# Attention and a linear layer on one core: the order in front of the first exponentials, the way the heads' output goes back, and the order of the last four heads

## The reference

```
Q, K, V = split_heads(xn @ wq.T), split_heads(xn @ wk.T), split_heads(xn @ wv.T)   # 16 heads of 8 channels
Q, K = rope(Q), rope(K)
scores = where(causal, Q @ K^T / sqrt(8), -inf)
attn = softmax(scores) @ V  ->  heads joined  ->  @ wo.T
linear = (xn @ CB.T) * (SCB / 127) + bias
out = x + attn + linear
```

## Time and profile before

| | |
|---|---|
| median of 3 runs | 279.49 us |
| the profiled execution | 278.35 us |
| its span | 276.6 us |
| PE busy | 242.5 us (88%) |
| DVE busy | 211.2 us (76%) |
| ACT busy | 187.0 us (68%) |
| POOL busy | 105.4 us (38%) |

### The profile page before, as it was taken

One profiled execution on the slowest core, in us unless ns is written; L12 is line 12 of the kernel. 1 busy time (PEld: TensorE's weight loads), 2 busy tenths in 40 slices (PEclk: granted clock), 3 DMA queues, 4 the chain that ended last, 5 costly groups with the idle time before them and its releaser, 6 DMA issues.

```text
span 276.6 us, 11045 instructions
## 1 busy us (share of the span) xinstructions
PE 242.5 (88%) x4736; PEld 125.3 (45%) x4736; DVE 211.2 (76%) x601; ACT 187.0 (68%) x366; POOL 105.4 (38%) x171
## 2 busy tenths in 40 slices
PE   0695788745989999999999999999999999999894
PEld 0342644103433544544455445445655444567552
DVE  5899277872899999989997899999998988414203
ACT  0425433403986789778779878986788898898741
POOL 7644992494703440492087014304301330430020
PEclk9999999955999999999999999999999999999999
DMA  7515857580004161016007001500800000000102
GB/s 202 187 28 142 213 125 140 120 207 4 4 1 117 41 154 28 4 46 133 7 4 164 14 4 46 134 2 15 162 9 4 4 5 4 5 23 25 43 21 59
DMA packets 21017, 18.29 MB, mean 66 GB/s; under 512 B 2516, under 2 KB 20308, under 8 KB 20968
## 3 DMA queue, kind: packets, MB, share of 16 engines
q1 hardware_dynamic: 20392, 17.00, 25.1%
q10 hardware_dynamic: 576, 0.59, 0.8%
HBM read 12.12 MB, written 5.24 MB: 63 GB/s over the span
## 4 chain that ended last, share of the span: by engine, by line
PE 63%; DVE 12%; POOL 8%; ACT 5%; DMA 5%; issue 3%; SPq 3%; ACTq 0%; POOLq 0%
PE psV L910 20%; PE psB L841 19%; PE psA L841 17%; DVE prod L743 7%; PE psA L945 4%; ACT ring L646 3%; DVE xn L701 2%; DMA k_scratch<-ot 2%; POOL x_sb L508 2%; POOL xnT L447 2%; POOL ot L440 2%; SPq L342 2%; PE psB L824 2%; DMA x_sb<-x 2%; SPq L356 1%
## 5 line engine op out<-in xcount | busy, mean ns | idle before, releaser
L743 DVE CUSTOM_DVE_ANT_0 prod<-psA,cmask 128x128 f32<-128x128 f32 (+7 forms) x256 | 179.2, 754 | 30.4 <-PE psA L841 28.3
L646 ACT ACTIVATE ring<-psB 128x512 f32<-128x512 f32 x288 | 154.7, 602 | 33.3 <-PE psB L841 29.8
L841 PE MATMUL psB<-qs,ks 128*32 128x512 bf16 (+3 forms) x1536 | 101.3, 329 | 1.8 <-ACT ring L646 0.9
L841 PE MATMUL psA<-ks,qs 128*32 128x512 bf16 (+3 forms) x1536 | 94.7, 334 | 6.3 <-DVE mx L743 3.7
L910 PE MATMUL psV<-ring,va 128*32 128x512 f32 (+3 forms) x768 | 75.9, 486 | 0.4 <-POOL ring L492 0.3
L492 POOL TENSOR_SCALAR_AFFINE_SELECT ring<-ring 128x512 f32<-128x512 f32 x64 | 39.5, 635 | 74.4 <-ACT ring L646 74.2
L841 PEld LDWEIGHTS psB<-qs,ks 128*32 128x32 bf16 x1536 | 41.0, 97 | 46.3 <-ACT ring L646 21.8
L841 PEld LDWEIGHTS psA<-ks,qs 128*32 128x32 bf16 x1536 | 34.7, 97 | 44.2 <-DVE mx L743 24.7
L910 PEld LDWEIGHTS psV<-ring,va 128*32 128x32 f32 x768 | 22.5, 110 | 16.0 <-issue 8.7
L472 POOL CAST shifts<-mx 128x16 bf16<-128x16 f32 x16 | 3.1, 196 | 63.5 <-DVE mx L743 63.5
L761 DVE RECIPROCAL rden<-psA 128x32 f32<-128x32 f32 x8 | 2.8, 354 | 24.3 <-PE psA L945 24.3
(11 more groups left out here) (80 smaller groups left out, 163.7 us busy)
## 6 DMA issues: line engine op xcount, KB each, us to landing
qs<-q_scratch SPq DMA_DIRECT2D x48, 96.0 KB
ks<-k_scratch SPq DMA_DIRECT2D x48, 96.0 KB
q_scratch<-ot SPq DMA_DIRECT2D x20, 128.0 KB, 2.5
k_scratch<-ot SPq DMA_DIRECT2D x12, 128.0 KB, 2.5
x_sb<-x SPq DMA_DIRECT2D x4, 256.0 KB, 4.8
rope_sb<-rope SPq DMA_DIRECT2D x2, 512.0 KB, 6.2
y<-xn SPq DMA_DIRECT2D x8, 128.0 KB, 1.8
w_sb<-weights ACTq DMA_DIRECT2D x1, 256.0 KB, 3.4
```

The costliest lines, as they stand in the source:

```text
L646: act.activation(ring[:, s % P_RING, k * HALF:(k + 1) * HALF], bank_b(e % B_RING), ACT.Exp)\
L743: last = dve.tensor_tensor_reduce(masked_scores[:, u % 2, at:at + w], psA[:, (u % 2) * SEQ + at:(u % 2) * SEQ + at + w], cmask[:, SEQ - w: ...
L841: mm = pe.matmul(psum[strip:strip + STRIP, at:at + size], keys[:, strip:strip + STRIP], queries, start=True, stop=True)
```

## The change

Four things are changed together.

1. **The front.** The late weights, scb and bias are loaded by SP behind the rope tables, not by ACT. PE runs 24 transposes of the identity first. DVE normalises tiles 8 to 15 only behind both rope rounds of batch 0. The scaling of the linear layer's weights comes ahead of POOL's third parts; the fill of ks slot 1 and the zeroing of `va` come behind them.
2. **The first exponentials.** Units 17 to 21 of quad 0 are put at places 1 and 4, the turn of its second half's maxima at place 7, quad 1's units start at place 7. The late rounds are spread over POOL's and ACT's lists by place (`LATE_SPLIT`, `LATE_BANK`), and POOL's splits have places of their own (`SPLIT_BANK`). All tables are new.
3. **Output through DRAM.** For both halves of batch 0 and the second half of batch 1, SP stores the saved [128 x 512] tile of each quad (`store_heads`), and loads the heads packed on 128 partitions and, by a broadcast read, their sums (`load_heads`, two DMAs). DVE makes one reciprocal and one product of 128x512, PE projects with 32 matmul records (`project_half`), DVE adds x. Only the last half, two groups, takes the old way. In PE's list `project_half` of the three stands at places 267, 288 and 292; the first turns of the last two groups stand at place 293.
4. **Quad 7** does its second half first.

```diff
-UNIT_BANK = [ [AHEAD x22], [0, 2, 5, 7, 8, 10, ...], [-4, ...], [-5, ...], [-8, ...], [-6, ...], [-4, ...], [-5, ..., 30] ]
+UNIT_BANK = [
+    [AHEAD x17, 37, 40, 40, 40, 40],
+    [7, 7, 9, 9, 9, 10, 11, 12, 12, 14, 15, 16, 17, 18, 19, 21, 21, 24, 25, 27, 28, 29],
...
+    [-11, -10, -9, -7, -6, -4, -2, 0, 0, 2, 2, 3, 6, 7, 8, 10, 12, 13, 15, 15, 16, 18],
...
+    [-7, -4, -4, -1, -1, 4, 6, 8, 10, 11, 14, 17, 18, 21, 23, 26, 27, 32, 32, 36, 38, 42],
 ]
 TURN_BANK = [
-    [AHEAD, AHEAD],
+    [AHEAD, 43],
...
-EARLY = {250: 0, 258: 1, 267: 2, 268: 3, 272: 4, 279: 5}
+SPLIT_BANK = [[-3, -1], [-8, -3], [-31, -16], [-29, -7], [-34, -14], [-39, -26], [-12, -6], [8, -12]]
+LATE_SPLIT = [[-2, 8, 14], [-2, 10, 17], [19, 30, 38], [22, 30, 40]]
+LATE_BANK = [[5, 12], [8, 14], [22, 32], [26, 34]]
+HALVES = [(0, 0), (0, 1), (1, ORDER[QUADS - 1][0])]
+LAST_HALF = ORDER[QUADS - 1][1]
+PROJECT_BANK = [267, 288, 292]
+TURN_FIRST = 293
+GROUPS = 2
...
+            def store_heads(i, hf):
+                h = HALVES.index((i // 4, hf))
+                sp.wait_ge(ot_saved, 2 * i + ORDER[i].index(hf) + 1)
+                rows = o_scratch[h, (i % 4) * QUAD:(i % 4 + 1) * QUAD, :, :].rearrange("j r t -> (j r) t")
+                sp.dma_start(rows, ot[:, i, hf * HALF:(hf + 1) * HALF]).then_inc(o_stored[h], 16)
+
+            def load_heads(h):
+                sp.wait_ge(o_stored[h], 16 * QUAD)
+                if h == 2:
+                    sp.wait_ge(half_filled, 1)
+                sp.dma_start(heads_t[:, h % 2, :], o_scratch[h, :, 0:DH, :]).then_inc(o_loaded[h], 16)
+                sp.dma_start(dens[:, h % 2, :], o_scratch[h, :, DH:DH + 1, :].to_broadcast([QUAD * QUAD, DH, HALF]))\
+                    .then_inc(o_loaded[h], 16)
...
             statistics(0)
             statistics(1)
             normalise(0)
+            normalise(1)
             statistics(2)
-            normalise(1)
             statistics(3)
-            normalise(2)
-            normalise(3)
...
+            for r in range(2):
+                rotate(2 * r)
+                rotate(2 * r + 1)
+                leave(2 * r)
+                leave(2 * r + 1)
+            normalise(2)
+            normalise(3)
...
+            def normalise_half(h):
+                dve.wait_ge(o_loaded[h], 2 * 16)
+                dve.reciprocal(dens[:, h % 2, :], dens[:, h % 2, :]).then_inc(dens_ready, 1)
+                dve.wait_ge(dens_ready, h + 1)
+                dve.tensor_tensor(heads_t[:, h % 2, :], heads_t[:, h % 2, :], dens[:, h % 2, :],
+                                  ALU.mult).then_inc(heads_ready, 1)
...
+            dve.wait_ge(part3, 8)
+            normalise_half(0)
+            normalise_half(1)
             dve.wait_ge(xb_ready, 8)
+            half_result(0)
+            half_result(1)
+            normalise_half(2)
+            half_result(2)
+            normalise_heads(0)
+            normalise_heads(1)
+            result(0)
+            result(1)
...
+            def project_half(h):
+                pe.wait_ge(a_drained, QUADS * NUNITS)
+                pe.wait_ge(heads_ready, h + 1)
+                for m in range(4):
+                    mm = turn_tile(half_bank(h)[:, m * P:(m + 1) * P], heads_t[:, h % 2, m * P:(m + 1) * P], w_sb[:, 5, :])
+                mm.then_inc(half_filled, 1)
...
+                if TURN_FIRST == n:
+                    for g in range(GROUPS):
+                        for m in range(2):
+                            turn(g, m, range(3))
```

More of the change, by code:

```diff
@@ L296, in attention_ffn_kernel @@
         ot_saved = sem("ot_saved")
+        o_stored = [sem(f"o_stored{h}") for h in range(3)]
+        o_loaded = [sem(f"o_loaded{h}") for h in range(3)]
+        dens_ready = sem("dens_ready")
+        heads_ready = sem("heads_ready")
+        half_filled = sem("half_filled")
         o_turned = sem("o_turned")
@@ L522, in rotate_all, with beside, masks @@
                     rotate(c, m)
[L524 to L546 removed]
+            def beside(n):
+                for i in range(QUADS):
+                    for hf in ORDER[i]:
+                        if NBANKS * i + SPLIT_BANK[i][hf] == n:
+                            split_maxima(i, hf)
+                for c in range(LATE, 2 * LATE):
+                    if LATE_SPLIT[c - LATE][0] == n:
+                        rotate_all(c)
+                for c in range(LATE, 2 * LATE):
+                    if LATE_SPLIT[c - LATE][1] == n:
+                        leave(c)
+                for c in range(LATE, 2 * LATE):
+                    if LATE_SPLIT[c - LATE][2] == n:
+                        third_part(c)
+            def masks(i, s):
+                for m in range(MASKS[i][s]):
+                    mask(i, s, m)
+                if STEPS[i][s][0] == D1 and STEPS[i][s][1] == 0:
+                    if ORDER[i][0] == 0:
+                        wait(pool, pv_done, i * NSTEPS)
+                        copy_v(i, 1)
+                if i == 1 and s == 2:
+                    for n in range(4):
+                        add_ffn(n)
+                if i == 2 and s == 2:
+                    for n in range(4):
+                        add_bias(n)
+            for n in (-3, -2, -1):
+                beside(n)
             for i in range(QUADS):
@@ L664, in beside @@
                 for i in range(QUADS):
-                    for hf in range(2):
+                    for hf in ORDER[i]:
                         if TURN_AT[i][hf] == n:
@@ L720, in leave, with rotate @@
                                   ALU.subtract).then_inc(rest1, 1)
-            for c in range(LATE):
+            def rotate(c):
                 r, w = divmod(c, 2)
@@ L926, in beside @@
                             values(i, s)
-            for n in range(FIRST_TASKS):
+            task(0, 0)
+            task(0, 1)
+            turn_rows(2)
+            turn_rows(3)
+            for n in range(1, FIRST_TASKS):
                 for m in range(2):
@@ L935, in _ @@
                         scores(i, u)
[L936 to L938 removed]
+                        for n in range(FIRST_TASKS, len(TASKS)):
+                            for m in range(2):
+                                if i == 0 and TASK_AFTER.get((n, m)) == u:
+                                    task(n, m)
             pe.wait_ge(task_saved, len(TASKS))
[L940 removed]
+            pe.wait_ge(va_set, 2)
             def turn_tile(to, tile, moving):
@@ L996, in _ @@
                         early(n)
-            for g in (GROUPS - 2, GROUPS - 1):
-                for m in range(2):
-                    turn(g, m, range(3))
-            for n in range(QUADS * NBANKS, QUADS * NBANKS + 16):
+            for n in range(QUADS * NBANKS, QUADS * NBANKS + 20):
                 beside(n)
+                early(n)
             for g in (GROUPS - 2, GROUPS - 1):
```

356 lines of the change are left out of this document (166 added, 190 removed), and 27 rows, old and new, of tables (UNIT_BANK, VALUE_BANK).

## The result

The changed kernel takes 283.97 us (282.44 to 291.13 in 4 runs) against 279.65 us of the kernel before in the same runs: ratio 1.013, 95% interval [1.009, 1.018]. It is slower, by less than the 2% that counts as a difference here. One of the four, 291.13, is a slow run and isn't in the ratio. The forecast was 272.5, its range 264 to 282. The profiled execution took 282.44 us, its span is 280.6 (276.6 before); it is the fastest of the four.

What follows compares the result with a forecast made beforehand. DVE was taken to bound the middle up to about 157 us, PE from there to 262. Stages of 149.8 + 98.0 + 22.5 gave a span of 270.3 us against 276.6, hence a time of 272.5, range 264 to 282.

Steps and rivals of the forecast that it cites:

- Step 1: Front up to quad 0's last maximum: earlier rope, tasks ahead of the units; it ends at 55.5 instead of 60.2 us.
- rival B: Normalises of tiles 8 to 15 beside POOL's third parts and fills take 6.4 us, not 2.2; time 275.8; chance 0.22.
- step 2: To the eleventh exponential: 3.8 us behind quad 0's last maximum, at 59.3 instead of 73.6 us.
- Step 3: Up to place 126, quads 1 to 4: DVE decides, 95% busy; reached at 149.8 instead of 155.4 us.
- rival C: POOL becomes the bound in the first quad, adding up to 12.2 us, time then 284.7 us; chance 0.13.
- Step 4: Place 126 to 283: PE is the bound and has less work; 98.0 us instead of 106.8.
- Step 5: Place 283 to the end: PE and everything wait for the trip through DRAM; 22.5 us instead of 14.4.

Runs made afterwards that it cites:

- experiment 1: The changed kernel, with POOL's three stack fills and zeroing of va waiting until DVE has normalised all 16 tiles: 279.76 us, ratio 0.999.
- experiment 3: The changed kernel with 96 more identity transposes on PE ahead of the turns of tiles 8 to 15: 283.11 us, ratio 1.013.
- experiment 4: The changed kernel with POOL's fills behind the normalises and 60 identity transposes ahead of the turns of tiles 8 to 15: 277.57 us, ratio 0.992.
- experiment 6: The changed kernel with PE's third project_half in psV behind the turns, DVE making the last two groups' heads behind the half's product: 283.64 us, ratio 1.016.
- earlier form of experiment 6: The changed kernel with PE's third project_half in psV behind the turns, but DVE's last heads ahead of the half's reciprocal: 284.64 us, ratio 1.015.
- experiment 5: The changed kernel with tiles 8 to 15 normalised ahead of rope, turned and copied earlier, and the last tasks some units later: 276.88 us, ratio 0.989.
- experiment 7: The changed kernel with front (normalises ahead of rope, earlier turns, later last tasks) and tail (third project_half behind the turns) both repaired: 274.0 us, ratio 0.980.

## Why the prediction was wrong

**Step 1 failed: quad 0's last maximum was to come at 55.5, and came at 68.4.** The first unit was 9.4 us late, and the units took 28.5 us in place of 25.0. The parts, after against forecast:

- Rests of round 1 end: 23.2 against 24.3. Rope did move forward as reasoned. That it was even 1.1 us better is luck of this execution: with the slower first projections of experiments 1, 3 and 4 the rests end at 24.8 to 26.0.
- "The normalises of tiles 8 to 15 are now behind all this": they were priced at 2.2 us, and took 9.8. This is the term that decided. It adds 7.6 us, 6.0 of them by the fills (experiment 1). The row was there: 3.21 us for four beside fills. The text used it for rival B only as a price for each normalise, 6.4 for eight, and did not ask how long the row of fills had become. In the kernel before those four met a fill of 0.95 us and one of 1.86 with a pause between; here four fills of 6.2 us stand together, since the change itself put ks slot 1 and `va` behind the third parts.
- PE's tasks ahead of the first unit: 7.0 us from the last normalise to the unit against 4.0, as PE had been idle and ran at half clock: at full clock it is 4.7 and 4.8 (experiments 3 and 4). The forecast looked at the clock only from 42 us on.
- The first six units: 13.3 us to the seventh at 53.2 against 8.2 forecast (38.7, or 9.2 to the 39.7 that the sum went on with). "Now the tasks are ahead of them" was a misreading: `TASK_AFTER` puts ten of these eleven tasks behind one or the other of the first six units. PE is the bound here, and not DVE: it is busy for all 15.20 us from 38.0 to 53.2, DVE for 7.11. From 39.88 on PE's records of the tasks make 10.5 us (4.04 of L890, 6.42 of L895), its score records 3.8. The kernel before had much the same tasks between its units, and from the first unit to the end of the last maximum it took 28.5 us (31.67 to 60.19), as the changed kernel did; the forecast had 25.0. This part stays when the front is repaired. There the eleventh is 7.3 us behind the forecast: 1.5 at the first unit, which waits for its stack (31.96 against 30.5), 4.6 in the first six units, 1.2 in step 2.
- The last 16 units: 15.2 us, forecast 15.8. DVE was busy for 15.18 of 15.20.
- The 24 transposes at the start kept PE busy for 5.4 us, not 0.9 to 1.8; it had no input yet, so that cost nothing.

**Step 2, the eleventh exponential: 5.0 us behind the last maximum, forecast 3.8.** A size: 1.2 too little. POOL's split came at once (68.48), the shifts' DMA was issued at 69.67, and 3.7 us from issue to exponential are more than the 2.5 that were left for it.

**Step 3 held, from its wrong start.** From the last maximum to place 126 the forecast had 94.3 us, measured 91.1. Its share for DVE was right. Window of the changed kernel, the maxima's line alone, beside the 91% of before:

```profile
68.00:158.00 90.00, 86.12 (x253) 1.00 0.34 81
```

96%, forecast 95%. Whether DVE alone decides is not told apart by it. With the late eleventh exponential the forecast's own terms give 158.0 for DVE without a pause (68.4 + 89.6) and 157.7 for PE (73.4 + 84.3), and PE is busy for 84.33 of the 86.1 us; place 126 came at 159.5. The stage was not longer than forecast, and POOL is busy for 44.05 of its 86.1 us: rival C, which added up to 12.2, had no part. Against the kernel before this stage costs 4.3 us, with more units in it; the repaired kernel pays 4.9.

**Step 4 held.** 99.4 against 98.0; before it was 106.8. Output through DRAM and the earlier units give 7.4 us here; no run has one without the other.

**Step 5 held.** 21.7 against 22.5. Timeline of the changed kernel:

```profile
259.98 0.32 SPq L400 DMA_DIRECT2D o_scratch<-ot  x1
261.99 0.58 SPq L407 DMA_DIRECT2D rot<-o_scratch  x1
266.78 3.35 DVE L805 RECIPROCAL rest<-rest 128x512 f32<-128x512 f32 x1 [1.18 <-DMA rest<-o_scratch]
271.00 1.93 PE L1019 MATMUL psA<-w_sb,rot 128*32 128x128 f32 x32 [6.17 <-DVE rot L807]
272.68 1.88 PE L1019 MATMUL psA<-ident,ot 128*32 128x36 f32 x128
```

Store 2.0 us to the loads' issue (2.7 forecast, the page has 2.4), 4.8 from there to the reciprocal (4.0), the reciprocal 3.35 (3.4), PE's idle hole 6.17 (6), and projection and turns at the lower clock, 3.8 together against 2.2 and the 1.5 added for it. From this place to the end it is 7.3 us more than before, so steps 4 and 5 together gave nothing: -7.4 and +7.3. What the forecast saw too was that the trip through DRAM waits at the end; it took that as given by the order, while the order of PE and DVE alone gives 2 us back (experiment 6).

The Trainium skill (VectorE: DVE Perf Modes, Walkthrough: the 8-slice pipeline in each mode) has a repeat count of 8 for a reciprocal, by which the estimate was 4.3 us. The run shows 3.35 for 512 columns, so the measurement stands against that estimate. That the row of 32 columns bears out either was a misreading: with the sum's own fixed part of 154 ns the estimate makes 421 ns of it, and the row has 354.

**Rival B, at 0.22, named the mechanism at about half its price** (4.2 us more for the normalises; it was 7.6). "If the first units start past 33, B holds": they started at 39.9. The Trainium skill (GPSIMD Engine Reference, its table of specifications) says that POOL's SBUF interfaces are shared with VectorE and contend with its two-port mode. The trace agrees in kind and goes further: the instruction was not slowed by a share, it stood still for the whole row of fills. PE waited 6.89 us for one that takes 0.28 (1.11 for four). That a normalise runs in such a mode is not shown by any run here.

**The range** ended at 282, though rival C in the same text gave 284.7 and 0.09 was put above 285.1. The upper end was cut short of the text's own rivals.

**What the change is worth in its parts**, by the repaired kernel against before (span 272.5 against 276.6): 7.0 us earlier at the eleventh exponential, with the early banks, 4.9 given back up to place 126, 7.4 won to place 283, 5.4 lost behind it, 4.1 in sum. As the change was written, its other front cost 6.8 of that at the eleventh exponential and its tail 1.9. The 6.8 is from a profiled execution whose first projections took 2.81 us; where they took 4.28 and 4.51, the same front had the eleventh at 75.1 and 75.7 (the earlier form of experiment 6, and experiment 6).

What stays open: that PE's tasks are the 4.6 us in the first six units is read from PE's busy time and from the equal 28.5 us before the change; no run took the tasks out. Why the granted clock is at its lower level during PE's first projections in most executions, and not in all, is not known. And whether a fill holds only normalises of this form was not measured by itself.

## What to carry to other kernels

When an instruction is moved to another time, look at what its neighbour engine does at that time, and price it by the longest unbroken row of it, not by one instance. A row of before in which an instruction takes three times its usual length is the thing to follow up, above all if the change makes its neighbour longer. Judge an experiment in one stage between two events of that stage, and not by its distance from the start, when something ahead of it varies between executions. Judge a change of several parts at checkpoints of the work (here the eleventh exponential, places 126 and 283): gains and losses of 4 to 7 us each added up to 4 us, and two small repairs turned it from 1.3% slower to 2% faster.

## What the runs showed of the hardware

- Of DVE's normalises (float32, SBUF to SBUF, 0.28 us each) one gets in between two of POOL's third parts of 1.1 us, and none while fills follow each other without a pause: held through four fills (25.55 to 31.73) and through two (29.74 to 33.28). Maxima out of PSUM run beside a fill at their usual 0.29 us.
- 96 transposes of the identity kept the granted clock up (1.00), at 10.64 us of PE time. The 24 at the start don't do it reliably: of eleven profiled executions that have them, the first six projections take 2.81 us in two (the changed kernel and experiment 5, granted clock 1.00 from 9.9 to 14.0 us) and 4.3 to 5.5 in the other nine (0.50 to 0.64); in the kernel before, without them, 4.07. The first exponential moves by up to 2.3 us between executions of the same front (61.7, 63.4, 64.0).
- 128 short matmul records in a row (11 ns each) ran for 94 and then stood for 2.96 us with nothing to wait for (experiment 6); the row breaks at the same record in its earlier form (2.86) and in experiment 7 (0.27). In each a packet of 16 KB of the instruction queue was moved shortly before PE went on, and PE went on 1.3 to 1.5 us behind its end: moved from 268.49 to 269.47 and on at 270.94 in experiment 6, 267.90 to 268.82 and 270.32 in its earlier form, 257.04 to 258.46 and 259.72 in experiment 7. In the first two it came later, among the loads that kept the DMA engines full. That the one is the cause of the other was not tested.
